# The place of the MLP's gelu in ScalarE's turn, in a four-stage transformer stack on one Trainium2 core

## The reference, cut to what matters

```python
def attn_layer(x, Wqkv, qs, ksc, Wo):        # 16 heads of 64, windows of 32 tokens
    q, k, v = split(x @ Wqkv)                # heads
    q = l2norm(q) * qs; k = l2norm(k) * ksc  # then the rotary factors on both
    sim = where(mask, -max, einsum(q, k of this and the previous window) * 8)
    return softmax(sim) @ v @ Wo

def ffn_layer(x, g, bln, W1, b1, W2, b2):    # hidden width 341
    xn = (x - mu) / sqrt(var + 1e-05) * g + bln
    a, gate = split(xn @ W1 + b1)
    return a * gelu(gate) @ W2 + b2

for i in range(6):
    x = attn_layer(shift_tokens(x), ...) + x
    x = ffn_layer(shift_tokens(x), ...) + x
```

## Time and profile before

| | us |
|---|---|
| median of 3 runs | 5601.84 (5597.76 to 5603.36) |
| the profiled execution | 5602.33 |
| its span | 5600.5 |
| PE busy | 4727.6 (84%) |
| PEld busy | 2816.1 (50%) |
| DVE busy | 3790.5 (68%) |
| ACT busy | 3328.5 (59%) |
| POOL busy | 2137.8 (38%) |

### The profile page before, as it was taken

The page is one execution under the profiler, slowest core; times in us unless marked ns, Lnnn a source line. Parts: engine busy times, 40 slices in busy tenths (PEclk is TensorE's granted clock), DMA queues, the critical chain, the costliest instruction groups (busy, mean ns, idle before and its releaser), DMA issues. The chain is left out here.

```text
span 5600.5 us, 128202 instructions
## 1 busy us (share of the span) xinstructions
PE 4727.6 (84%) x48610; PEld 2816.1 (50%) x48610; DVE 3790.5 (68%) x5402; ACT 3328.5 (59%) x5608; POOL 2137.8 (38%) x1085
## 2 busy tenths in 40 slices
PE   1596597698699999999999934977999999999997
PEld 0232243243366666666666612334666666666664
DVE  1764465471588888888888626616888888888884
ACT  0154364366277777777777610654777777777774
POOL 2000000000366565656565320005655656565651
PEclk6798798899699999999999967997999999999998
DMA  4102202200000000000000031000000000000000
GB/s 78 14 13 26 38 2 37 37 1 1 29 9 9 14 9 14 9 14 9 14 9 6 1 57 21 1 29 9 9 2 18 6 18 6 14 9 14 9 6 9
DMA packets 67925, 88.13 MB, mean 16 GB/s; under 512 B 20608, under 2 KB 42236, under 8 KB 66812
## 3 DMA queue, kind: packets, MB, share of 16 engines
q1 hardware_dynamic: 67408, 80.92, 7.3%
HBM read 66.49 MB, written 13.63 MB: 14 GB/s over the span
## 5 line engine op out<-in xcount | busy, mean ns | idle before, releaser
L679 DVE TENSOR_REDUCE a_nm<-ps 128x128 f32 (+7 forms) x768 | 558.5, 755 | 376.5 <-PE ps L632 361.3
L903 PE MATMUL ps<-l_wqk,l_xa 128*128 128x512 f32 x1536 | 766.8, 623 | 46.8 <-DVE l_rs L1349 40.1
L1010 PE MATMUL ps<-l_yb,l_mh 128*128 128x256 f32 x3072 | 710.1, 381 | 0.0
L699 ACT ACTIVATE a_pt<-ps 128x512 f32<-128x512 f32 (+3 forms) x1152 | 509.0, 501 | 331.7 <-PE ps L649 251.5
L1306 POOL TENSOR_TENSOR l_pn<-l_pe,l_rl 128x1024 f32<-128x1024 f32 x192 | 365.2, 1902 | 616.7 <-DVE l_rl L1387 613.8
L1010 PEld LDWEIGHTS ps<-l_yb,l_mh 128*128 128x128 f32 x3072 | 564.5, 190 | 71.5 <-issue 2.4
L1150 ACT ACTIVATE l_sq<-ps 128x1024 f32<-128x1024 f32 x384 | 389.8, 1015 | 316.6 <-PE ps L903 316.6
L628 PE MATMUL ps<-a_ks,a_qs 128*128 x1152 | 322.6, 342 | 271.3 <-DMA a_ks<-scratch 218.8
L601 POOL COPY a_vq<-a_vrow 128x256 f32 x24 | 9.6, 400 | 1306.7 <-PE ps L660 692.1
L1349 DVE TENSOR_TENSOR l_rs<-ps,l_tab 128x512 f32<-128x512 f32 x768 | 491.0, 681 | 0.0
L1289 POOL TENSOR_TENSOR l_rc<-l_rc,l_rs 128x1024 f32<-128x1024 f32 x192 | 451.6, 2352 | 44.4 <-DVE l_rs L1349 44.4
(11 more groups left out here) (215 smaller groups left out, 9315.8 us busy)
## 6 DMA issues: line engine op xcount, KB each, us to landing
l_wqk<-in_lWqkv SPq DMA_DIRECT2D x24, 512.0 KB, 3.8
scratch<-a_ot SPq DMA_DIRECT2D x12, 768.0 KB, 4.7
a_qs<-scratch SPq DMA_DIRECT2D x36, 256.0 KB
a_ks<-scratch SPq DMA_DIRECT2D x36, 256.0 KB
l_wvt<-in_lWvT SPq DMA_DIRECT2D x12, 512.0 KB, 4.8
l_wo<-in_lWo SPq DMA_DIRECT2D x12, 512.0 KB, 7.0
l_w<-in_lW SPq DMA_DIRECT2D x12, 341.0 KB, 2.9
scratch<-b_ot SPq DMA_DIRECT2D x4, 768.0 KB, 13.9
```

Of the source, the lines that this page charges most:

```text
L679: nc.vector.tensor_reduce(nm[:, bass.ds(quad * 32 + j * QT + qt, 1)], flat1[:, 0:P * (qt + 1)], AX.X, ALU.max, negate=True).then_inc(s1_fr ...
L699: nc.scalar.activation(pt[:, x % 2, j, 0:w], ps[:, S2_BANKS[seen2 % (3 if now else 6)], 0:w], ACT.Exp).then_inc(s2_free, 1)
L903: last = nc.tensor.matmul(ps[:, x, :], xa[:, u, o:o + P], wqk[:, a * INNER + x * CH:a * INNER + (x + 1) * CH], start=True, stop=True)
L1010: last = nc.tensor.matmul(ps[:, 6, 0:2 * P], mh[:, h, :], yb[:, n % 2, h, :], start=h == 0, stop=h == LH - 1, skip_group_check=True)
```

## The change

ACT's `gelu(i)` moves from behind `ln_deviation(i)` to the place in front of `exponentials(i+1)`. Nothing else is changed in the source.

```diff
--- before.py
+++ after.py
@@ -1257,12 +1257,12 @@
                                 ln_square(i)
                                 place_k(i + 2)
                                 take_head_weights(i, 1, 0)
+                                gelu(i)
                                 exponentials(i + 1)
                                 square_qk(i + 4, 0)
                                 place_p(i)
                                 deviations(i + 3)
                                 ln_deviation(i)
-                                gelu(i)
                                 take_head_weights(i, 0, 1)
                                 take_head_weights(i, 1, 1)
                                 take_mixed(i, 0)
```

## The result

The changed kernel takes 5780.24 us (median of 4 runs, 5771.02 to 5792.24) against 5599.80 us of the kernel before (4 runs): ratio 1.0323, 95% interval 1.0303 to 1.0343. The change costs 180 us, and the time lies inside the forecast's range of 5715 to 5800 us. The profiled execution took 5792.24 us, with a span of 5790.5 us, 190.0 more than that of before.

The account below looks back on a forecast made before the run. PE was taken to bound the layers; first 44 x 1.45, second 44 x 0.85, third 34 x 1.49 + 10 x 0.76, less 2 and half of 2.6, gave +156.2 us on 5602.3: 5758 us, range 5715 to 5800.

Parts of the forecast that it names:

- PE bounds the layers, and what counts is what makes it wait: In the layers PE, busy 1164.29 of 1200 us, sets the time; only what makes it wait can cost.
- The exponentials 1.99 us later, and nothing hides it: On ACT, load (1.28), gelu (0.69) and 0.02 us between delay the exponentials by 1.99 us, all of it exposed.
- `other` is relieved by what `mix(i, 0)` loses: On PE, `other` saves its 0.57 us gelu wait, `mix(i, 0)` waits about 0.5 us for probabilities; the two cancel.
- DVE's chain has a slack of 0.54, 1.14 and 0.50 us: DVE's copy before `mix(i, 1)`: delay beyond slack costs 1.45, 0.85, 1.49 us in first, second, third gelu turns.
- The ten head-weight turns: Ten third gelu turns where DVE's copy waits for `mix(i, 0)`: 0.76 us each at `mix(i, 1)`.
- The clock would stay: PE's granted clock stays at 1.00 behind waits of 2 us, as between 1558 and 1640 us; no cost.
- Rival F: PE would be granted its lower clock level in turns with a wait of 2 us; chance 0.02.
- The next turn starts in step: DVE's 2.26 and POOL's 2.49 us idle absorb their delays; the next turn begins only later, deviation turns cost nothing.
- The sum: Gelu turns 63.8, 37.4 and 58.3, less 2, together 157.5 us; less half of 2.6 for loads: +156.2 us.
- late subtractions: Where exponentials already wait for DVE's subtraction (5.8 us over 192), part of the new work fits in: 2 us off.
- the two table loads less: On ACT, one table load less in each call takes off at most 2.6 us; half was counted.
- the forecast's main path: Late exponentials delay DVE's chain to its first copy, for which `mix(i, 1)` waits: 1.45, 0.85, 1.49 us per turn.

Follow-up runs that it names:

- e3: Kernel before, with the gelu replaced by a plain pass with the same bias (no table load), at its old place: 5533.23 us, ratio 0.9864.
- e1: Changed kernel, but in the ten third gelu turns that are head-weight turns the gelu stays behind the square roots: 5751.04 us, ratio 1.0260.
- e10: The changed kernel run once more, nothing altered, to look at its stretches at the lower clock: 5788.32 us, ratio 1.0323.
- the copy ahead: DVE's `take_mixed(i, 0)` moved ahead of the reciprocal norms: in the changed kernel 5728.51 us, in the kernel before 5620.84 us.
- e5: Kernel before, with `gelu(i)` moved directly behind `exponentials(i + 1)`: 5740.12 us, ratio 1.0263.
- e6: Kernel before, with `gelu(i)` moved behind `place_p(i)`, ahead of the square roots: 5746.12 us, ratio 1.0275.

## Why the prediction was right, and where not

*PE bounds the layers, and what counts is what makes it wait:* right. PE's share went from 97% to 92% as forecast.

*The exponentials 1.99 us later, and nothing hides it:* right; 2.00 in the trace. Putting the load at its 1.31 us by the row, and not at the page's 2.66 (ScalarE: Activation LUTs of the Trainium skill, the same section), was right as well: in the rows above load and gelu delay the exponentials by 2.00 us, not by 3.35.

*`other` is relieved by what `mix(i, 0)` loses:* right for the outcome. `mix(i, 0)` waits 0.51 us, and PE's waiting ahead of `other`, 0.57 us, is gone. e3 shows that this was worth 0.84 us at `mix(i, 1)` and not 0.57, so PE alone would have been early; since DVE's copy ends later, that changed nothing.

*DVE's chain has a slack of 0.54, 1.14 and 0.50 us:* right for the first and third turns, which cost in the median what was forecast to 0.01 us, 59.1 and 52.5 us in sum against 63.8 and 50.7. In the second turns the term was mis-sized: 0.56 us instead of 0.85. The sentence that failed is "everything from there to the end of `take_mixed(i, 0)` at 2019.54 runs without a gap". The copy at 2018.78 started 0.05 us behind the end of `mix(i, 0)`, at 2018.73; it waited for PE, in a gap too short to be seen. This is the instruction ahead of it on DVE, in the kernel before:

```profile
2018.38 0.35 DVE L1367 RECIPROCAL l_rn<-l_rn 128x32 f32<-128x32 f32 x1
```

The reciprocal ends at 2018.73 as well, 0.05 us ahead of the copy; in the changed kernel, where `mix(i, 0)` ended at 2045.65, 1.32 us ahead of the copy, the copy starts 0.08 us before the reciprocal ends, and takes 0.69 us instead of 0.76. In the median second turn it ends 6.04 us behind the start of the exponentials, and not 6.34. So the chain by itself is 0.3 us shorter, and its slack was 1.44. In 44 turns that is 13 us less; in the sum it shows as 6, since some second turns cost up to 1.6 us.

*The ten head-weight turns:* wrong, forecast 0.76 us each and measured 3.63 in the median, in sum 8 and 36. I looked only at what `mix(i, 1)` waits for and took the probabilities' delay for settled with `mix(i, 0)`. But it has a second reader in these turns, line 1019, which had been waiting 0.87 us for it before, so that all of the delay went through: 1.99 us in each, 20 us in all. e1 shows that these turns alone hold the whole 36 us.

*The clock would stay:* wrong by some 16 us, all that the head-weight turns have beyond 1.99 us each, and by 1.7 us in each of two turns ahead of the first gelu. Rival F was turned down with the waits of about 2.3 us at a full clock. The new waits at `mix(i, 1)` are near that length, up to 2.5 us, and the clock stays at 1.00 behind all of them in this trace, and behind all but one in e10's. The one that I had not seen is longer.

*The next turn starts in step:* right for the change; the turns with deviations cost 0.00 us in the median. It is not a matter of course, as the copy ahead shows.

*The sum:* 156 us forecast. The trace has 190: 29 more in the head-weight turns, 6 less in the second turns, 3 less in the first and third, 2 that had been taken off for late subtractions, 1.3 for the two table loads less (line 1198 has 190 instead of 192, and no gain from it is to be seen), and 10 more outside the gelu turns, of which 1.7 us twice are again a low clock and the rest I have not explained. The medians of the runs have 180. So the forecast's main path carried it: 143 of the 190 us are in the first, second and third turns, where it had 152. What it had missed, the head-weight turns' second wait and the clock behind it, was about a seventh.

## What to carry to other kernels

When an instruction is made late, list every reader of what it and its followers on that engine write, in the rare turns too: a reader that already waits takes the whole delay, one with slack only the rest, and here ten rare turns (36 us) outweighed the 44 second ones (31). Slack is start of the reader less end of the writer, and it has to be read for the chain as it would run alone; a step that begins 0.05 us behind another engine's end may have been waiting, whatever the idle column says. A load of ACT's tables took 1283 ns in each place of these traces, so put it where what is queued behind it has the slack.

## What I had not expected of the hardware

A wait can cost more than itself. These are the longer waits within the layers in five traces (the changed kernel twice, e1, e5 and e6), and how often a stretch at 1.2 GHz came behind them, mostly worth another 1.65 us, sometimes 3.4:

| weight loads' idle time | waits | with a low stretch |
|---|---|---|
| 2.2 to 2.55 us | 225 | 1 |
| 2.64 to 2.72 us (e6) | 35 | 5 |
| 2.86 us (head-weight turns) | 30 | 21 |
| 2.9 to 3.0 us (e6) | 37 | 24 |

Two waits that are harmless apart, joined into one, cost more: with the gelu behind the probabilities' copy (e6) a low stretch came in 22 of 32 turns with deviations, and with the wait split in two (e5) in none. The same waits brought a low stretch in one execution and none in another, so that the length alone does not decide it.
